# Attention scores with the queries stationary, and values laid out block-diagonally, in a conditioned transformer block

## The reference, cut to what matters

```python
def _tc_rmsnorm(x, t, gw, gb, bw, bb):
    g = (t @ gw.T + gb)[:, None, :]
    b = (t @ bw.T + bb)[:, None, :]
    inv_rms = rsqrt(mean(x * x, axis=-1, keepdims=True) + EPS)
    return g * x * inv_rms + b

def _attention(x, Wq, Wk, Wv, Wo):               # 16 heads of 16 channels
    q, k, v = (x @ W.T).reshape(B, L, 16, 16) ...
    p = softmax(einsum('blhd,bmhd->bhlm', q, k) / 4, axis=-1)
    o = einsum('bhlm,bmhd->blhd', p, v).reshape(B, L, D)
    return o @ Wo.T

y = x + _attention(_tc_rmsnorm(x, t, g1...), ...)
y = y + (silu(n @ gate_w.T) * (n @ hid_w.T)) @ out_w.T    # n = _tc_rmsnorm(y, t, g2...), hidden 1024
out = x + y
```

## Time and profile before

| | |
|---|---|
| median of 3 runs | 991.04 us (990.25 to 996.09) |
| the profiled execution, span | 991.4 us |
| PE busy | 954.4 us (96%) |
| PE weight loads busy | 817.3 us (82%) |
| DVE busy | 661.2 us (67%) |
| ACT busy | 561.7 us (57%) |
| POOL busy | 447.6 us (45%) |
| mean granted PE clock | 0.983 |

### The profile page before, as it was taken

How to read it: one execution, slowest core, us unless ns; L and a number is a source line. 1 busy time by engine, 2 the same in 40 slices (tenths; PEclk the granted TensorE clock), 3 DMA queues, 4 the chain that set the end, 5 groups by cost and what they waited for, 6 DMA issues and landing times.

```text
span 991.4 us, 24429 instructions
## 1 busy us (share of the span) xinstructions
PE 954.4 (96%) x9112; PEld 817.3 (82%) x9112; DVE 661.2 (67%) x1178; ACT 561.7 (57%) x1271; POOL 447.6 (45%) x393
## 2 busy tenths in 40 slices
PE   6679999999999999999999999999999999999788
PEld 5568888889888898888889888888978888897767
DVE  3856777676777757676675767667576776757552
ACT  6645556565655655565465566646556565655342
POOL 4355345254534535454453545435354552535242
PEclk9688999999999999999999999999999999999999
DMA  5100010000100000010000101000010100000000
GB/s 183 45 1 22 2 38 8 22 21 0 42 0 22 20 21 21 0 42 0 21 21 5 37 0 42 0 21 21 0 42 0 42 0 21 21 0 22 2 22 22
DMA packets 18971, 21.71 MB, mean 22 GB/s; under 512 B 640, under 2 KB 18240, under 8 KB 18816
## 3 DMA queue, kind: packets, MB, share of 16 engines
q1 hardware_dynamic: 18720, 21.24, 6.4%
q10 hardware_dynamic: 224, 0.10, 0.1%
HBM read 12.95 MB, written 8.39 MB: 22 GB/s over the span
## 4 chain that ended last, share of the span: by engine, by line
PE 90%; DVE 3%; ACT 2%; POOL 2%; issue 2%; DMA 1%; DVEq 0%; POOLq 0%; ACTq 0%
PE ps L1051 10%; PE ps L1053 9%; PE ps L1052 9%; PE ps L1143 7%; PE ps L1200 6%; PE ps L1184 6%; PE ps L1151 6%; PE ps L1203 5%; PE ps L1201 5%; PE ps L1192 5%; PE ps L1185 5%; PE ps L1173 3%; PE ps L1077 3%; PE ps L1080 3%; PE ps L1078 3%; PE ps L1069 2%
## 5 line engine op out<-in xcount | busy, mean ns | idle before, releaser
L264 POOL TENSOR_TENSOR h_lo<-h,h_hi 128x512 fp32r<-128x512 f32 x128 | 165.3, 1291 | 251.8 <-ACT h_hi L462 251.8
L270 POOL TENSOR_TENSOR probs<-probs,recip 128x512 f32<-128x512 f32 x128 | 132.8, 1047 | 48.0 <-DVE recip L776 47.8
L1051 PE MATMUL ps<-out_w_hi,h_hi 128*128 128x256 f32 x512 | 150.1, 293 | 0.9
L1053 PE MATMUL ps<-out_w_hi,h_lo 128*128 128x256 f32 x512 | 144.6, 282 | 0.0
L1052 PE MATMUL ps<-out_w_lo,h_hi 128*128 128x256 f32 x512 | 144.2, 282 | 0.0
L799 DVE SCALAR_TENSOR_TENSOR shared<-shared,ps 128x512 f32<-128x512 f32 x128 | 87.4, 683 | 74.9 <-ACT shared L457 74.3
L457 ACT ACTIVATE shared<-ps 128x512 f32<-128x512 f32 x128 | 76.8, 600 | 100.0 <-PE ps L1192 96.4
L1184 PE MATMUL ps<-xn_hi,gate_w_hi 128*128 128x512 f32 x256 | 108.9, 425 | 1.2 <-ACT xn_hi L431 0.8
L1200 PE MATMUL ps<-xn_hi,hid_w_hi 128*128 128x512 f32 x256 | 106.1, 414 | 0.1
L1051 PEld LDWEIGHTS ps<-out_w_hi,h_hi 128*128 128x128 f32 x512 | 96.6, 189 | 11.7 <-POOL h_lo L264 7.3
L472 ACT COPY probsT<-ps 128x512 f32<-128x512 f32 x128 | 73.7, 589 | 56.1 <-PE ps L1151 55.5
(11 more groups left out here) (92 smaller groups left out, 2152.6 us busy)
## 6 DMA issues: line engine op xcount, KB each, us to landing
x_in<-in_x SPq DMA_DIRECT2D x16, 512.0 KB, 3.4
out<-result SPq DMA_DIRECT2D x15, 512.0 KB, 3.0
shared<-in_attT SPq DMA_DIRECT2D x1, 1024.0 KB, 6.8
shared<-in_gateT SPq DMA_DIRECT2D x1, 1024.0 KB, 8.7
shared<-in_hidT SPq DMA_DIRECT2D x1, 1024.0 KB, 4.8
shared<-in_outT SPq DMA_DIRECT2D x1, 1024.0 KB, 6.8
out<-result SPq DMA_DIRECT2D x2, 256.0 KB, 2.2
result<-in_modT SPq DMA_DIRECT2D x1, 256.0 KB, 4.8
```

Of the source, the lines that this page charges most:

```text
L264: nc.gpsimd.tensor_tensor(h_lo[:, j % KEPT, :], h[:, j % 2, :], h_hi[:, j % KEPT, :].bitcast(F32), ALU.subtract).then_inc(h_lo_done, 1)
L270: nc.gpsimd.tensor_tensor(own, own, recip[:, p % TOGETHER, :].unsqueeze(2).to_broadcast([P, SEQS, L]), ALU.mult).then_inc(divided, 1)
L1051: nc.tensor.matmul(dst, a_hi, b_hi, start=first, stop=False, skip_group_check=skip)
L1053: return nc.tensor.matmul(dst, a_lo, b_hi, start=False, stop=last, skip_group_check=skip)
```

## The change

- `scores` takes the 64 queries of a sequence (32 x 64) as the stationary operand, and as the moving one 128 columns: that sequence's keys once masked for each head of the pair. The mask with its factor 1/4 moves from `queries` to `keys`: keys take two instructions on each engine, queries one. The result has queries on 64 partitions, and the two sequences of a block go to the two halves of the partitions, side by side. Columns are (block, head, key).
- `values` becomes block-diagonal: for each sequence and pair 128 rows (head, key) by 32 columns (head, channel), where only the two blocks on the diagonal are filled. POOL clears it once at the start. Each of ACT and DVE fills one sequence of every block (ACT the first, DVE the second), for both heads, two instructions each, and both now wait for both halves of the projection.
- `values_probs` multiplies 128 rows x 32 columns with 64 moving columns (one sequence's queries); the result is the attention itself, in one bank a round (`att_bank`). `first_heads`, `second_heads`, `own_head` and `attT` go. `high_attention` and `low_attention` (one instruction) read PSUM; what waited for `attT_done` waits for `attT_lo_done`.
- In the orders: ACT's `first_values(t + 1)` moves from after tanh 7 to after `scale_second(t)`; DVE's `second_values(t + 1)` from after `first_residual` to after hidden 7, ahead of `scale_second_rest`; DVE's `low_attention(t, 0)` stands after `scale_rows(t + 1)`, where `second_heads(t, 0)` stood ahead of it. ACT's `high_attention(t, 0)` takes the place of `first_heads(t, 0)`. Tile 0 and tile 15 are changed in the same sense, without values at the end of tile 15.

The diff, cut to the steps named in this document:

```diff
@@ -99,15 +98,16 @@
         xn1_lo = sb("xn1_lo", [P, CH, TOK], F32R)
-        queries = sb("queries", [P, CH, SEQS, 2, L])
-        keys = sb("keys", [P, CH, TOK])
-        values = sb("values", [P, BLK, D])
+        queries = sb("queries", [P, CH, TOK])
+        keys = sb("keys", [P, CH, SEQS, 2, L])
+        values = sb("values", [P, SEQS, PAIRS, ROWS])
         row_max = sb("row_max", [P, TOGETHER, SEQS])
...
         probsT = sb("probsT", [P, TOGETHER, TOK])
-        attT = sb("attT_sum", [P, TOK])
         attT_hi = sb("attT_hi", [P, 2, TOK], F32R)
@@ -187,12 +187,20 @@
         def v_bank(u, half):
-            return (GATE, Y)[half] if alone(u) else PAIR + half
-        def heads_of(r, head):
-            return ps[:, PAIR + 2 * r:PAIR + 2 * r + 2, :].rearrange(
-                "p s (k h q) -> p (s k) h q", h=2, q=L)[:, :, head, :]
+            return Y + half if alone(u) else PAIR + half
+        def att_bank(r):
+            return PAIR + 2 * r
+        def values_of(u, seq, head):
+            return ps[seq * L:(seq + 1) * L, v_bank(u, 0):v_bank(u, 0) + 2, :].rearrange(
+                "p a (k n h d) -> p (a k) n h d", k=2, h=2, d=DH)[:, :, :, head, :]
+        def value_rows(seq, head):
+            return values[head * L:(head + 1) * L, :, :, :].rearrange(
+                "p (k s) n c -> p k s n c", s=2)[:, :, seq, :, head * DH:(head + 1) * DH]
         block = ctx.enter_context(nc.Block())
@@ -433,23 +442,26 @@
             def first_keys(u):
                 act.wait_ge(k_mm, CH * u + 1)
-                nc.scalar.copy(keys[:, 0, :], ps[:, k_bank(u, 0), :]).then_inc(k_act_done, 1)
+                for head in range(2):
+                    last = nc.scalar.activation(keys[:, 0, :, head, :],
+                                                ps[:, k_bank(u, 0), :].rearrange("p (b q) -> p b q", q=L), ACT.Copy,
+                                                scale=head_mask[:, head:head + 1])
+                last.then_inc(k_act_done, 1)
             def first_queries(u):
                 act.wait_ge(q_mm, CH * u + 1)
+                nc.scalar.copy(queries[:, 0, :], ps[:, q_bank(u, 0), :]).then_inc(q_act_done, 1)
+            def first_values(u):
+                act.wait_ge(v_mm, 2 * u + 2)
+                wait(act, pv_mm, ROUNDS * u)
+                if alone(u):
+                    act.wait_ge(zeros_set, 1)
                 for head in range(2):
-                    last = nc.scalar.activation(queries[:, 0, :, head, :],
-                                                ps[:, q_bank(u, 0), :].rearrange("p (b q) -> p b q", q=L), ACT.Copy,
-                                                scale=head_mask[:, head:head + 1])
-                last.then_inc(q_act_done, 1)
-            def first_values(u):
-                act.wait_ge(v_mm, 2 * u + 1)
-                wait(act, pv_mm, ROUNDS * u)
-                nc.scalar.copy(values[:, 0:2, :], ps[:, v_bank(u, 0), :].rearrange("p (k n) -> p k n", k=2)
-                               ).then_inc(v_act_done, 1)
+                    last = nc.scalar.copy(value_rows(0, head), values_of(u, 0, head))
+                last.then_inc(v_act_done, 1)
             def tanh(u, j):
@@ -471,18 +483,10 @@
                 nc.scalar.copy(probsT[:, p % TOGETHER, :], ps[:, bank_of(t, p), :]).then_inc(probsT_done, 1)
-            def first_heads(t, r):
+            def high_attention(t, r):
                 act.wait_ge(pv_mm, ROUNDS * t + r + 1)
-                wait(act, attT_lo_done, ROUNDS * t + r)
-                nc.scalar.activation(attT.rearrange("p (b q) -> p b q", q=L),
-                                     heads_of(r, 0), ACT.Copy, scale=own_head[:, 0:1]).then_inc(attT_first, 1)
-            def high_attention(t, r):
-                act.wait_ge(attT_done, ROUNDS * t + r + 1)
                 wait(act, proj_mm, 2 * t)
-                nc.scalar.copy(attT_hi[:, r, :].rearrange("p (k s q) -> p s k q", s=2, q=L),
-                               attT.rearrange("p (s k q) -> p s k q", s=2, q=L)).then_inc(attT_hi_done, 1)
+                nc.scalar.copy(attT_hi[:, r, :], ps[:, att_bank(r), :]).then_inc(attT_hi_done, 1)
             mean_squares(0, x_in, x_loaded, (16, 16), x_scaled1, xT1_done, ms1, ms1_done)
@@ -637,7 +637,7 @@
                 if attend:
-                    first_heads(t, 0)
+                    high_attention(t, 0)
                 if ahead:
@@ -658,23 +658,21 @@
                 if attend:
-                    high_attention(t, 0)
                     keep_transposed(t, 6)
...
                 if attend:
-                    first_heads(t, 1)
                     high_attention(t, 1)
...
                     tanh(t - 1, 7)
-                if ahead:
-                    first_values(t + 1)
                 if mlp:
...
                     scale_second(t)
+                if ahead:
+                    first_values(t + 1)
                 if mlp:
@@ -734,23 +732,26 @@
             def second_keys(u):
                 dve.wait_ge(k_mm, CH * u + 2)
-                nc.vector.tensor_copy(keys[:, 1, :], ps[:, k_bank(u, 1), :]).then_inc(k_dve_done, 1)
-            def second_queries(u):
-                dve.wait_ge(q_mm, CH * u + 2)
                 for head in range(2):
                     last = nc.vector.tensor_scalar(
-                        queries[:, 1, :, head, :], ps[:, q_bank(u, 1), :].rearrange("p (b q) -> p b q", q=L),
+                        keys[:, 1, :, head, :], ps[:, k_bank(u, 1), :].rearrange("p (b q) -> p b q", q=L),
                         head_mask[:, head:head + 1], None, ALU.mult)
-                last.then_inc(q_dve_done, 1)
+                last.then_inc(k_dve_done, 1)
+            def second_queries(u):
+                dve.wait_ge(q_mm, CH * u + 2)
+                nc.vector.tensor_copy(queries[:, 1, :], ps[:, q_bank(u, 1), :]).then_inc(q_dve_done, 1)
             def second_values(u):
...
                 wait(dve, pv_mm, ROUNDS * u)
-                nc.vector.tensor_copy(values[:, 2:4, :], ps[:, v_bank(u, 1), :].rearrange("p (k n) -> p k n", k=2)
-                                      ).then_inc(v_dve_done, 1)
+                if alone(u):
+                    dve.wait_ge(zeros_set, 1)
+                for head in range(2):
+                    last = nc.vector.tensor_copy(value_rows(1, head), values_of(u, 1, head))
+                last.then_inc(v_dve_done, 1)
             def row_maxima(t, p):
@@ -775,23 +776,11 @@
                 nc.vector.reciprocal(recip[:, p % TOGETHER, :], sums[:, p % TOGETHER, :]).then_inc(recip_done, 1)
-            def second_heads(t, r):
-                dve.wait_ge(attT_first, ROUNDS * t + r + 1)
-                dst = attT.rearrange("p (b q) -> p b q", q=L)
-                nc.vector.scalar_tensor_tensor(dst, heads_of(r, 1), own_head[:, 1:2], dst,
-                                               ALU.mult, ALU.add).then_inc(attT_done, 1)
             def low_attention(t, r):
...
                 wait(dve, proj_mm, 2 * t)
-                by_seq = "p (k s q) -> p s k q"
-                for seq in range(2):
-                    last = nc.vector.tensor_tensor(
-                        attT_lo[:, r, :].rearrange(by_seq, s=2, q=L)[:, seq, :, :],
-                        attT.rearrange("p (s k q) -> p s k q", s=2, q=L)[:, seq, :, :],
-                        attT_hi[:, r, :].rearrange(by_seq, s=2, q=L)[:, seq, :, :].bitcast(F32), ALU.subtract)
-                last.then_inc(attT_lo_done, 1)
+                nc.vector.tensor_tensor(attT_lo[:, r, :], ps[:, att_bank(r), :], attT_hi[:, r, :].bitcast(F32),
+                                        ALU.subtract).then_inc(attT_lo_done, 1)
             def silu(u, j):
@@ -995,10 +980,10 @@
                     silu(t - 1, 5)
-                if attend:
-                    second_heads(t, 0)
                 if ahead:
                     scale_rows(t + 1, x_in, inv1, inv1_done, x_scaled1, xT1_done, scaled1)
+                if attend:
+                    low_attention(t, 0)
                 if mlp:
@@ -1023,21 +1008,19 @@
                     reciprocals(t, 7)
-                    low_attention(t, 0)
                 if ahead:
...
                 if attend:
-                    second_heads(t, 1)
                     low_attention(t, 1)
...
                     first_residual(t)
-                if ahead:
-                    second_values(t + 1)
                 if mlp:
...
                     hidden(t - 1, 7)
+                if ahead:
+                    second_values(t + 1)
                 if attend:
@@ -1105,7 +1088,10 @@
             def project_v(u, half, probs_of=None):
-                pe.wait_ge((k_act_done, k_dve_done)[half], u + 1)
+                if not alone(u):
+                    pe.wait_ge((k_act_done, k_dve_done)[half], u + 1)
+                elif half == 0:
+                    pe.wait_ge(k_dve_done, 1)
                 for k in (2 * half, 2 * half + 1):
@@ -1135,14 +1121,16 @@
                 else:
```

(29 more changed lines are left out.)

34 lines of the change are left out of this document (13 added, 21 removed).

## The result

The changed kernel takes 995.29 us (median of 20 runs, 991.83 to 996.72), the kernel before 992.49 us (20 runs): a ratio of 1.0022 (of the means), 95% interval 1.0012 to 1.0032. The forecast was 988 us and slightly faster; the time is 7 us above it, inside the range, and the kernel is slightly slower. Device time is not the span, though the text on the kernel before takes the two as one: it is 1.8 us above it here (991.83 us for a span of 990.0) and 2.0 us above it in another execution of the kernel before (993.51 for 991.5). A forecast summed on the span alone sits some 2 us low.

What follows compares the result with a forecast made beforehand. PE was taken to set the pace, with little room in the other engines' chains. Per tile -0.6 - 0.45 + 1.2 = +0.15 us, fourteen tiles +2, ends -5.5, from 991.4 to 988 us; own range 980 to 1000, outer range 976 to 1006.

Steps and rivals of the forecast that it cites:

- end of the tile: DVE's two values copies between hidden 7 and scale_second_rest delay the norm's transposes, PE standing 1.2 us a tile.
- front of the tile: From scores 0 to values 0: silu 0 and hidden 0 come sooner, 0.6 us a tile arriving at the values products.
- Scores matmuls: A scores round on PE, eight parts at once, takes 1.05 us instead of 1.94; gross gain 0.9 us a round.
- Values matmuls: A values round on PE takes 1.1 us, nothing gained; weight loads hidden behind products in the same rows.
- the third rival: Weight loads of the values products are not hidden: +0.4 us twice a tile, 1001 us; chance 0.11.
- Second scores: DVE's low attention half stands behind scaling: second scores start 0.45 us late, so 0.45 of their 0.9 us gain is left.
- Below 1.2 nothing suggests itself: Lower bound for the cost of the two values copies at the end of the tile: not below 1.2 us.
- the upper bound of 1.8: Values copies at the tile's end cost 1.8 us if writes in runs of 16 are half as fast again.
- First and last tile: First tile gains 4 us, last tile 1.5 us; POOL's memset of the values falls in its wait for the input.
- The sum: Per tile +0.15 us, fourteen tiles +2, ends -5.5: 991.4 - 3.4 = 988 us.
- (1): Rival: the halves take turns, scores rounds stay at 1.94 us and the delays stay: 1012 us; chance 0.12.
- The faster one (2): Rival: front gives 0.9 us, low half does not wait for scaling, or low-clock stretches shorten: 977 us; chance 0.21.

Runs made afterwards that it cites:

- experiment 5: Changed kernel with the eight sequences of a scores round taken in the order 0, 2, 4, 6, 1, 3, 5, 7: 998.71 us, ratio 1.0061.
- experiment 4: Changed kernel with DVE's low_norm2(t - 1) moved ahead of results(t - 2) at the start of a tile: 1008.0 us, ratio 1.0157.
- experiment 8: Experiment 7 with DVE's results(t - 2) moved from ahead of low_norm2(t - 1) to behind hidden(t - 1, 0): 978.38 us, ratio 0.9853.
- experiment 11: Changed kernel with DVE's values copies written to their own tile in one plain run of 512, odd sequences left out of attention: 993.98 us.
- experiment 12: Changed kernel with DVE's values copies read plainly and written plainly to their own tile, odd sequences left out of attention: 993.61 us.
- experiment 1: Changed kernel with DVE's second_values moved behind scale_second_rest: 979.64 us, ratio 0.9867.
- experiment 2: Changed kernel with DVE's second_values placed between silu 7 and hidden 7: 979.82 us, ratio 0.9865.
- experiment 6: Kernel before with only DVE's second_values (one instruction) moved behind hidden 7, ahead of scale_second_rest: 1001.87 us, ratio 1.0091.
- experiment 7: Changed kernel with DVE's second_values between silu 7 and hidden 7 and ACT's first_values behind the last high half: 974.88 us, ratio 0.9817.
- experiment 3: Changed kernel with DVE's low_attention(t, 0) moved ahead of scale_rows(t + 1): 994.35 us, ratio 1.0012.
- experiment 9: Experiment 7 with POOL's inverse_rms(t + 1) ahead of low_hidden 3 and DVE's four scale instructions ahead of silu 5: 967.43 us, ratio 0.9749.
- experiment 10: Experiment 9 with eight more products of 512 columns, result unused, in a wait of the first tile: 967.22 us, ratio 0.9741.

## Why the prediction was wrong, point by point

The mechanisms came as forecast, and the sizes of two terms did not. The step that failed is the end of the tile: its two copies were put at 1.2 us, and the time between the last values products and the norm's transposes grew by 1.49 us, 0.29 us more in each of fourteen tiles, 4 us in all. Without these 4 us the kernel would have come out slightly faster (an estimate: 995.3 - 4.1 = 991.2 us, against 992.5). The front of the tile, put at -0.6 us, gave -0.41 us, another 2.7 us. Besides, the sum was made on the span and on one clock.

**Scores matmuls: right.** 1.05 us was forecast, 1.12 measured. That eight parts work at once in the 32x64 form was an inference from the values' 64x32 form, and experiment 5 shows it: four records in 0.109 us in one half, eight in 0.11 in both. The Trainium skill (TensorEngine Tiling (Array Packing), Available Configurations) lists this form with eight parts, and the runs agree.

**Values matmuls: right.** 1.1 forecast, 1.03 measured: four records start every 0.056 us, each with its weight load. A load of 110 ns is in flight while products run in the same 128 rows. By the Trainium skill (TensorE: Matmul & The Clock Gate, The mechanism) loads overlap only where the row group differs; the same section also excepts loads into the background weight buffer, and no record tells which buffer a load goes to. For a plain reading of the rule the trace does not agree, and the third rival is out.

**Front of the tile: right in mechanism, too large.** silu 0 came where forecast. From there the working let hidden 0 follow silu 0 directly. Its matmul was late: gate 0's low part waits for the norm's low half (543.11 to 543.59 in PE's rows, where 0.23 is the step), and hid 0 stands behind it. 0.41 us arrived, not 0.6. The norm's low half on DVE ends 0.54 to 0.56 us behind POOL's whenever it begins, so neither of the two orders tried on DVE (experiments 4 and 8) moved it.

**Second scores: right.** 0.39 late for 0.45 forecast, 0.82 won for 0.9.

**End of the tile: right in place, too small; this is the step that failed.** "Two copies of 512 elements (0.69 us each, 0.61 from start to start)" was taken from a full-height copy. Full-height DVE instructions here start 0.08 us before the end of the one ahead where nothing holds them. These do not: hidden 7 to copy 0.72 us, copy to copy 0.71, copy to scaling 0.72, in place of 0.61 each. Three steps of 0.1 us make 1.54 us of the 1.2, some 0.3 us a tile. "Below 1.2 nothing suggests itself" held; the upper bound of 1.8 was for another reason, runs of 16, and experiments 11 and 12 rule that reason out. That the copies' place makes the stall is shown by experiments 1, 2 and 6; why each step takes 0.1 us more stays open between height and start partition.

**First and last tile.** 4 us forecast ahead of tile 1's scores, 3.45 measured. POOL's memset of the values takes 1.80 us and lies in its wait for the input, as forecast. The last tile gave 4.2 us, not 1.5: before, its project_out waited 3.0 us for the low attention half, after 1.4, which I had read in the first tile only. There the loss of the head sums does pay. But about 1.3 us of each of the two gains is the clock of the profiled execution and no merit of the change, as the sum below shows.

**The sum.** Thirteen tiles lose 0.5 us each more than forecast, 6.5 us; the tile ahead of them gains 2.3 more than forecast, the ends 2.2. So the span is 2.0 us longer than forecast, 990.0 and not 988; that it is no more is luck in part, the 1.3 us twice told of below and a clock stretch that no term had (see rivals). Device time is 1.8 us above the span, which I had left out by setting the span beside the median. The last 3.5 us, from 991.8 to 995.3, go with the mean granted clock, 0.991 in the profiled run and 0.986 in most others. Only the profiled run has a trace, but those of the experiments suggest where most of the 3.5 us lie. In tile 0 the granted clock is at 0.50 in several stretches. One of them ends at 44.4 to 45.5 us in experiments 1, 2, 4, 7, 8 and 11, and there the scores of tile 1 start at 70.4 to 71.1 us. In the profiled run and in 3, 5, 9, 10 and 12 it ends at 42.0 to 43.2 us, and they start at 69.3 to 69.7 us. From the last scores round to the end, experiments 1, 2, 7, 9, 10, 11 and 12 take 72.3 to 72.5 us, with 3.4 us at 0.50 from some 27 us behind that round on; the profiled run has no such stretch and takes 71.1. That is 1.3 us twice, 2.6 of the 3.5. What decides which clock a run gets stays open.

**Rivals.** The halves do not take turns (1), loads are hidden (3). The faster one (2) did not come about as a whole. One part of it did: the clock is at 0.50 from 69.5 to 72.9 us, where it was so from 71.0 to 81.3 in the kernel before (and from 70.3 to 80.5 in experiment 6, which has its products too), and the 2.1 us that tile 1 gained go with it (from its scores 0 to its values 0 it takes 21.73 us and not 24.91). The rest came once the order was mended: experiment 9 is 2.5% faster than before. Of the 1.64 us of PE work saved a tile, the change as made gave back 1.49 at the norm and 0.39 at the second scores, and 0.41 never got past DVE.

## What to carry to other kernels

In this kernel one engine is full and three are half full, and the cut on the full one was worth nothing until the order on the others was looked at: the same new products cost 0.2% with two copies ahead of a scaling and gain 1.8% with them moved into waits, 2.5% with the next wait mended too. Before putting a step ahead of another, ask who waits for the second one, and price the step by an instruction of its own height and form, its start-to-start time included. And a shorter stretch of work hides less: what was free behind 1.9 us of scores is not free behind 1.1.

## What the runs showed of the hardware

- A DVE copy of 64 x 512 out of PSUM takes as long as one of 128 x 512 (0.69 us). These copies, which change the start partition too, do not overlap their neighbours: +0.01 to +0.03 us from end to start, where full-height instructions have -0.08. Plain or stepped, it is the same (experiments 11 and 12).
- With the halves apart (experiment 5), the products of the second half seem to start some 20 records into the block of 32 of the first, by the rate of the starts.
- DVE's low half of the norm (L730) takes 0.55 us plus the time by which it overlaps POOL's own: 0.73 us with 0.19 of overlap (the first in the loop), 0.87 with 0.33 (the changed kernel), 1.05 with 0.50 (experiment 9), 1.26 with 0.71 (experiments 4 and 8). By these rows it makes no headway while POOL's runs. In experiment 9 four scale instructions take 1.93 us and not 1.13; the first of them lasts 1.14 us, 0.99 of it beside POOL's low half of the hidden layer, and the others 0.34:

```profile
546.60 1.93 DVE L693 TENSOR_SCALAR x_scaled<-x_in,inv 128x256 f32<-128x256 f32 x4
...
545.30 1.02 POOL L256 TENSOR_TENSOR inv<-mse,minus_half 128x4 f32<-128x4 f32 x1 [0.16 <-POOL mse L253]
546.29 1.30 POOL L273 TENSOR_TENSOR h_lo<-h,h_hi 128x512 fp32r<-128x512 f32 x1
```
